# Layer 1's expert rest of 32 rows stacked in one matmul, biases seeded in two copies, splits held and fillers added

## The chip, the cores and the metric

The kernel runs on one core of a Trainium2 chip. The metric is the device time of one execution in microseconds. Three runs of the kernel before took 590.12, 591.79 and 592.01, median 591.79. The engines are named as the profile names them: PE (matmul), ACT (scalar), DVE (vector), POOL (GpSimd), SP (queues DMAs).

## The reference, cut to what matters

The input is 1536 tokens of 256 channels. Two layers follow each other; each is an attention-like block and a mixture of eight experts with two experts per token:

```python
x = x + L0_conv(_ln_c(x)); t = t + L0_ffn(_ln_t(t))      # layer 0
x = x + L1_conv(_ln_c(x)); t = t + L1_ffn(_ln_t(t))      # layer 1
# layer 0's expert e:   y = silu(xf @ w1[e] + b1[e]) @ w2[e] + b2[e]          hidden 1024
# layer 1's expert e:   a, g = split(x @ W1[e] + b1[e], 2)                      2 x 672
#                       y = (a * silu(g)) @ W2[e] + b2[e]                       hidden 672
# out += y * weight of e for the token, for the two chosen experts
```

Everything is float32. The change concerns mostly layer 1's experts, whose hidden width is 672: six times 112, or five times 128 and 32 more.

## The kernel before, in words

Each layer first loads and normalises the tokens, transposes them on PE, computes values and scores, softmax and projection (the conv stage), adds the result to `xres`, normalises again (`xn2`), routes every token to two experts on DVE, and builds tables: 1536 x 2 token rows are sorted by expert into blocks of 128 rows, in layer 1 here 28 blocks. Then a loop runs over the blocks.

A block's rows are gathered from DRAM by POOL (`gather`), transposed on PE (`x_transpose`), and split by ACT and DVE into a high part and a low rest (`xT_hi`, `xT_lo`), since the matmuls run on a shorter float type: each product is three matmuls, high by high, high by low, low by high (`product`, lines 1249 to 1251). All expert weights are split the same way into `w_hi` and `w_lo`. The first three experts of a layer are split ahead of the loop, in 12 pieces, high part by ACT (`high_pieces`, L663) and low part by POOL (L582); later experts within the loop, in pieces, by ACT (L804) and DVE (L1144).

On PE, `step(b)` does in this order: transposes of block b+1's rows; the second product of block b-1 (L1463 on); the transposes of block b's hidden values (`h_transpose`, L1457); the first product of block b+1. In layer 1 the hidden 672 columns are transposed as six tiles of 112, so a second product is 6 x 3 = 18 matmuls of 256 columns. The output bias rides in tile 0 as a 113th row. The first product adds onto PSUM banks which ACT has filled with the bias b1 (`seed`, L794): one copy of 4 x 336 columns in layer 1, which waits until the previous block's `h` is made. Layer 1's first product goes through chunks 2, 3 (the gate g), then 0, 1.

ACT's step: two copies of the transposed hidden values (`hT_hi`), two SiLUs, `xT_hi`, the seed, pieces of the weight split. DVE's step: two `hT_lo`, two products `h_sb` (L1214), `xT_lo`, the block's output `y` (L1231), pieces of the split. POOL's step: gather of block b+2, then scatter-add of block b-1's `y` to DRAM, each scatter waiting for the one before.

PE matmuls on zeros (`keep_busy`, L1257) stand at several places of the routing. At the end of layer 0 the last two blocks are added by one-hot matmuls (`last_rows`, L1504; their one-hots are made on DVE in `last_onehot`, L1184 and L1188), while POOL already splits expert 0 of layer 1 (L582). In each layer's conv stage, DVE multiplies `x_logits` (L1008) before it adds the projected rows (L1016).

## Time and profile before

| what | us |
|---|---|
| median of three runs | 591.79 |
| profiled execution | 593.63 |
| its span | 591.9 |
| PE busy | 544.1 (92%) |
| DVE, ACT, POOL busy | 338.6, 333.3, 280.2 |
| layer 0's loop, first hidden transposes to last | 101 to 284 |
| layer 1's loop, first hidden transposes to last | 389 to 576 |

The profile is of one execution. Busy PE time overstates, since consecutive matmuls overlap; the distance between starts is what one costs in a row of them. A row of the timeline gives start, duration, engine, line, operation, tiles and shape, how many were merged, and in brackets the idle time before it with what ended it.

### The profile page before, as it was taken

Reading aid. Unit: us, or ns where it says so; the run is one execution under the profiler, and the core shown is the slowest. Engines: PE = TensorE matmul, PEld = TensorE weight load, DVE = VectorE, ACT = ScalarE, POOL = GpSimd, SP = SyncE. Lnnn points to the kernel's source line nnn. Section 1 sums busy time; section 2 is a strip of 40 time slices with the busy share of each in tenths; the row PEclk is TensorE's granted clock in tenths of the full one; section 3 lists DMA queues with packets and bytes.
Section 4 is the critical chain, followed back from the end, with each engine's and each line's share of the span. In section 5 each row is a group of like instructions: output and inputs, shape, how many; then the busy total and the mean of one; then the engine's idle time right before and its main releaser. Section 6 shows DMA issues by size and latency. Waiting matters only on the chain.

```text
span 591.9 us, 15435 instructions
## 1 busy us (share of the span) xinstructions
PE 544.1 (92%) x3572; PEld 479.0 (81%) x3573; DVE 338.6 (57%) x719; ACT 333.3 (56%) x605; POOL 280.2 (47%) x331
## 2 busy tenths in 40 slices
PE   7999858999999999999789998699999999999991
PEld 3797525999999989998678874389999999999891
DVE  5448985455544555564884578744655565656330
ACT  3688324566755667665447755254666665666430
POOL 4448214346554466653814260425446555545422
PEclk9799988999999999999999999799999999999996
DMA  7435567455642444235431246532264555322110
GB/s 265 136 107 153 171 210 228 119 150 139 155 83 35 114 123 96 41 88 166 150 100 57 89 144 213 196 120 37 60 193 127 137 137 138 71 76 37 30 27 10
DMA packets 48122, 69.96 MB, mean 118 GB/s; under 512 B 8790, under 2 KB 39648, under 8 KB 48096
## 3 DMA queue, kind: packets, MB, share of 16 engines
q1 hardware_dynamic: 34304, 55.88, 29.4%
q0 software_dynamic: 10464, 13.58, 13.1%
q10 hardware_dynamic: 3328, 0.20, 0.3%
q8 instruction: 12, 0.20, 0.2%
q14 instruction: 14, 0.11, 0.1%
HBM read 57.01 MB, written 13.47 MB: 119 GB/s over the span
## 4 chain that ended last, share of the span: by engine, by line
PE 64%; DMA 13%; DVE 11%; issue 4%; ACT 3%; POOL 3%; POOLq 1%; SPq 0%; DVEq 0%; ACTq 0%
PE banks L1249 14%; PE banks L1251 14%; PE banks L1250 14%; DMA mid_dram<-expert_io,scol 10%; PE banks L1288 5%; PE banks L1457 5%; PE banks L1362 2%; DVE stats L872 2%; PE banks L1426 2%; DVE onehot_row L1095 2%; POOL expert_io L614 2%; PE banks L1257 1%; DVE x_logits L1008 1%; PE banks L1299 1%; DMA xres<-in_x_dram 1%
## 5 line engine op out<-in xcount | busy, mean ns | idle before, releaser
L1249 PE MATMUL banks<-w_hi,xT_hi 128*128 x336 | 119.5, 356 | 4.6 <-DVE xT_lo L1135 2.6
L1249 PE MATMUL banks<-w_hi,hT_hi 128*128 (+2 forms) x392 | 115.8, 295 | 2.0 <-DVE hT_lo L1204 1.3
L1251 PE MATMUL banks<-w_hi,xT_lo 128*128 x336 | 114.9, 342 | 0.0
L1250 PE MATMUL banks<-w_lo,xT_hi 128*128 x336 | 114.3, 340 | 0.0
L1251 PE MATMUL banks<-w_hi,hT_lo 128*128 (+2 forms) x392 | 110.8, 283 | 0.0
L1250 PE MATMUL banks<-w_lo,hT_hi 128*128 (+2 forms) x392 | 110.8, 283 | 0.0
L582 POOL TENSOR_TENSOR w_lo<-raw,w_hi 128x1024 fp32r<-128x1024 f32 (+1 forms) x24 | 62.0, 2604 | 55.8 <-ACT w_hi L663 55.8
L794 ACT COPY banks<-seed_rows 128x1024 f32 (+1 forms) x56 | 64.4, 1151 | 31.0 <-issue 13.5
L1249 PEld LDWEIGHTS banks<-w_hi,hT_hi 128*128 128x128 f32 (+2 forms) x392 | 74.8, 191 | 4.7 <-issue 3.6
L1250 PEld LDWEIGHTS banks<-w_lo,hT_hi 128*128 128x128 f32 (+2 forms) x392 | 75.1, 192 | 0.0
L1251 PEld LDWEIGHTS banks<-w_hi,hT_lo 128*128 128x128 f32 (+2 forms) x392 | 74.9, 191 | 0.0
L602 POOL DMA_INDIRECT expert_io<-xn_dram,gcol x52 | 52.6, 1012 | 41.7 <-POOL gcol L598 40.1
L1204 DVE TENSOR_TENSOR hT_lo<-banks,hT_hi 128x512 fp32r<-128x512 f32 (+1 forms) x112 | 64.4, 616 | 12.2 <-ACT hT_hi L818 7.4
L1249 PEld LDWEIGHTS banks<-w_hi,xT_hi 128*128 128x128 f32 x336 | 63.2, 188 | 8.9 <-issue 5.5
L818 ACT CAST hT_hi<-banks 128x512 fp32r<-128x512 f32 (+1 forms) x112 | 54.1, 535 | 26.1 <-PE banks L1457 23.7
L1251 PEld LDWEIGHTS banks<-w_hi,xT_lo 128*128 128x128 f32 x336 | 63.0, 188 | 4.7
L1250 PEld LDWEIGHTS banks<-w_lo,xT_hi 128*128 128x128 f32 x336 | 63.4, 189 | 3.5
L831 ACT ACTIVATE h_sb<-banks 128x512 f32<-128x512 f32 x56 | 33.5, 599 | 57.0 <-PE banks L1251 57.0
L1144 DVE TENSOR_TENSOR w_lo<-raw,w_hi x40 | 50.3, 1265 | 17.7 <-issue 17.7
L617 POOL DMA_INDIRECT out_dram<-expert_io,scol x27 | 44.1, 1632 | 25.4 <-POOL expert_io L614 23.8
L617 POOL DMA_INDIRECT mid_dram<-expert_io,scol x26 | 43.4, 1670 | 23.1 <-POOL expert_io L614 23.1
L1457 PE MATMUL banks<-ident,h_sb 128*128 128x128 f32 (+1 forms) x392 | 51.9, 272 | 0.0
(206 smaller groups left out, 899.4 us busy)
## 6 DMA issues: line engine op xcount, KB each, us to landing
raw<-in_L_ffn_w_dram SPq DMA_DIRECT2D x32, 512.0 KB, 4.0
raw<-in_L_ffn_W_dram SPq DMA_DIRECT2D x16, 672.0 KB, 4.1
raw<-in_L_ffn_W_dram SPq DMA_DIRECT2D x16, 336.0 KB, 3.8
seed_rows<-in_L_ffn_b_dram SPq DMA_DIRECT2D x8, 672.0 KB
seed_rows<-in_L_ffn_b_dram SPq DMA_DIRECT2D x8, 512.0 KB
xn_dram<-raw SPq DMA_DIRECT2D x6, 512.0 KB, 3.0
wqkv<-in_L_conv_W_qkv_dram SPq DMA_DIRECT2D x2, 768.0 KB, 5.6
mid_dram<-xres SPq DMA_DIRECT2D x3, 512.0 KB, 4.0
```

Source lines behind the costliest of these rows:

```text
L582: pool.tensor_tensor(w_lo[:, e, at], raw[:, 0, at], w_hi[:, e, at].bitcast(F32), ALU.subtract).then_inc(s.pool_split, 1)
L602: pool.indirect_dma_start(out=xg if after(b, 1) else xg_first, out_offset=None, in_=xn_dram, in_offset=bass.IndirectOffsetOnAxis(ap=rows, ...
L617: pool.indirect_dma_start(out=acc, out_offset=bass.IndirectOffsetOnAxis(ap=scol[:, :], axis=0), in_=y_out, in_offset=None, bounds_check=TO ...
L794: nc.scalar.copy(banks[:, 0:f.chunks, 0:f.chunk], seed_row(L, e % SLOTS)[:, 0:f.wide].rearrange("p (c n) -> p c n", c=f.chunks)).then_inc( ...
L818: nc.scalar.copy(hT_hi[0:f.kh, half * j:half * (j + 1), :], bank[4 + j][0:f.kh, 0:half * P].rearrange("p (k s) -> p k s", s=P)).then_inc(s ...
L831: nc.scalar.activation(h_sb[:, f.chunk * j:f.chunk * (j + 1)], bank[j][:, 0:f.chunk], ACT.Silu).then_inc(s.h, 1)
L1144: nc.vector.tensor_tensor(w_lo[:, slot, at], raw[:, (q // PIECES) % 2, at], w_hi[:, slot, at].bitcast(F32), ALU.subtract).then_inc(s.w_lo, 1)
L1204: nc.vector.tensor_tensor(hT_lo[0:f.kh, part, :], bank[4 + j][0:f.kh, 0:half * P].rearrange("p (k s) -> p k s", s=P), hT_hi[0:f.kh, part, ...
L1249: pe.matmul(out, hi, w_high, start=first, stop=False, skip_group_check=onto)
L1250: pe.matmul(out, hi, w_low, start=False, stop=False, skip_group_check=onto)
L1251: return pe.matmul(out, lo, w_high, start=False, stop=last, skip_group_check=onto)
L1457: mm = pe.transpose(bank[4 + j][0:f.kh, k * P:(k + 1) * P], h_sb[:, o:o + f.kh], ident[:, :])
```

## The change

1. Layer 1's hidden width is cut into five tiles of 128 and a rest of 32. The rest's tile is stacked: rows 0 to 31 and 64 to 95 hold the high part, rows 32 to 63 its low rest, rows 96 and 97 ones; the weights beside it hold high, high, low, and the bias as high and low. One matmul of 98 rows then does what three did. `hT_hi`'s two copies take 2 and 4 tiles in place of 3 and 3; DVE repeats the last 32 columns of `h` twice more, and writes the low rows. Each weight piece of the loop's split gets a small second instruction on ACT and on DVE.
2. Layer 1's bias is seeded in two copies of 2 x 336 columns; that for chunks 2 and 3 waits for the SiLUs alone.
3. POOL's splits: pieces 10 and 11 of either layer wait until `x_logits` is made; layer 1's first piece waits for the last one-hot and the end of layer 0's experts.
4. Five matmuls on zeros after the second group of transposes at the start of layer 0.
5. Three more DMAs per expert of layer 1 (the 32 rows three times, the bias row twice); four shared semaphores for the loads of x; register loads moved.

```diff
+BUSY_CHUNK = 5
+HELD_SPLIT = 10
-FFN = [Ffn(wide=1024, kt=8, kh=128, chunk=512), Ffn(wide=1344, kt=6, kh=112, chunk=336)]
+FFN = [Ffn(wide=1024, full=8, tail=0, first_tiles=4, chunk=512), Ffn(wide=1344, full=5, tail=32, first_tiles=2, chunk=336)]
+STACK_LOW, STACK_BIAS_LOW, STACK_ROWS = 64, 96, 98
...
+        def piece_parts(L, q, low):
+            tail_words = C if FFN[L].tail else 0
+            w = (WORDS[L] - tail_words) // PIECES
+            parts = [(slice(0, P), bass.ds((q % PIECES) * w, w))]
+            if tail_words:
+                n = C // PIECES
+                rows = slice(STACK_LOW, STACK_BIAS_LOW + 1) if low else slice(0, STACK_ROWS)
+                parts.append((rows, bass.ds((q % PIECES) * n + PIECES * w, n)))
+            return parts
...
                     pool.wait_ge(s.first_hi, q + 1)
+                    if q == HELD_SPLIT:
+                        pool.wait_ge(x_part, L + 1)
+                    if L == 1 and q == 0:
+                        pool.wait_ge(last_hot, 4)
+                        pool.wait_ge(lay[0].moe_done, 1)
...
-                def seed(b, e):
+                def seed(b, e, pair):
+                    chunks = slice(2 * pair, 2 * pair + 2)
                     act.wait_ge(seed_in, e + (E * L + 1))
                     if after(b, 1):
-                        act.wait_ge(s.h, 2 * b)
+                        act.wait_ge((s.h, s.silu)[pair] if L else s.h, 2 * b)
...
                     if L == 1:
-                        e_next = expert_of(b + 1)
+                        seed(b + 1, e_next, 1)
                         pieces = piece_range(act, b)
                     xT_high(b + 1)
-                    seed(b + 1, e_next)
+                    seed(b + 1, e_next, 0)
...
+                            if f.tail and j == 1:
+                                rows = slice(f.tail, 2 * f.tail)
+                                nc.vector.tensor_tensor(hT_hi[rows, f.full, :], bank[5][rows, 3 * P:4 * P],
+                                                        hT_hi[rows, f.full, :].bitcast(F32), ALU.subtract)
...
+                            if j == 1:
+                                again = STACK_BIAS_LOW // f.tail - 1
+                                nc.vector.tensor_tensor(
+                                    h_sb[:, f.hidden:f.hidden + again * f.tail].rearrange("p (r n) -> p r n", r=again),
...
+                    if L == 0 and j == 1:
+                        keep_busy(BUSY_CHUNK, 6)
...
-                    for k in range(f.kt):
-                        if k % half == 0:
-                            pe.wait_ge(s.hT_lo, 2 * b + 1 + k // half)
-                        rows = f.kh + (f.bias_row if k == 0 else 0)
-                        mm = product(bank[6][:, 0:C], hT_hi[0:rows, k, :], hT_lo[0:rows, k, :], high[0:rows, k, :],
-                                     low[0:rows, k, :], k == 0, k == f.kt - 1)
+                    for k in range(f.full):
+                        for j in range(2):
+                            if k == f.tiles[j].start:
+                                pe.wait_ge(s.hT_lo, 2 * b + 1 + j)
+                        mm = product(bank[6][:, 0:C], hT_hi[:, k, :], hT_lo[:, k, :], high[:, k, :], low[:, k, :],
+                                     k == 0, k == f.kt - 1)
+                    if f.tail:
+                        mm = pe.matmul(bank[6][:, 0:C], hT_hi[0:STACK_ROWS, f.full, :], high[0:STACK_ROWS, f.full, :],
+                                       start=False, stop=True)
```

## Rows read from the trace of the kernel before

**Rows 1.** The page's first two parts: busy time, and granted clock in 40 slices.
```profile
PE 544.1 (92%) x3572; PEld 479.0 (81%) x3573; DVE 338.6 (57%) x719; ACT 333.3 (56%) x605; POOL 280.2 (47%) x331
PEclk9799988999999999999999999799999999999996
```
**Rows 2.** PE's groups by shape: busy us, mean ns, idle before.
```profile
L1249 PE MATMUL banks<-w_hi,hT_hi 113*128 x28 | 10.4, 371 | 0.7 <-issue 0.7
```
**Rows 3.** Timeline of PE, one block of layer 1's loop.
```profile
414.72 0.36 PE L1249 MATMUL banks<-w_hi,hT_hi 113*128 x1
...
416.72 0.28 PE L1250 MATMUL banks<-w_lo,hT_hi 112*128 x1
416.84 0.28 PE L1251 MATMUL banks<-w_hi,hT_lo 112*128 x1
416.96 0.82 PE L1457 MATMUL banks<-ident,h_sb 128*112 128x128 f32 x6
```
**Rows 4.** Timeline of DVE and ACT, a block of layer 1 with two split pieces.
```profile
458.88 2.42 DVE L1144 TENSOR_TENSOR w_lo<-raw,w_hi  x2 [0.44 <-issue]
461.22 1.01 DVE L1204 TENSOR_TENSOR hT_lo<-banks,hT_hi 112x384 fp32r<-112x384 f32 x2
```
**Rows 5.** Timeline of POOL, two scatters of layer 1, eleven blocks apart.
```profile
435.48 1.59 POOL L617 DMA_INDIRECT out_dram<-expert_io,scol  x1 [0.91 <-POOL expert_io L614]
508.22 1.68 POOL L617 DMA_INDIRECT out_dram<-expert_io,scol  x1 [0.91 <-POOL expert_io L614]
```
**Rows 6.** Busy time by stretch of layer 1's loop (us, PE, PEld, DVE, ACT, POOL, PEclk, DMA share, GB/s).
```profile
430.43:505.48 75.05, 75.04 (x553) 73.92 (x552) 44.34 (x77) 47.45 (x78) 41.77 (x56) 1.00 0.55 147
```
**Rows 7.** Timeline of layer 1's blocks 0 to 1: DVE, ACT, PE.
```profile
389.12 0.42 DVE L1135 TENSOR_TENSOR xT_lo<-banks,xT_hi 128x256 fp32r<-128x256 f32 x1 [1.12 <-ACT xT_hi L784]
388.99 1.28 ACT L794 COPY banks<-seed_rows 128x1344 f32 x1
390.58 0.41 PE L1249 MATMUL banks<-w_hi,xT_hi 128*128 x1 [1.24 <-ACT banks L794]
```
**Rows 8.** Timeline of layer 0's conv stage: POOL, DVE, PE.
```profile
46.73 15.69 POOL L582 TENSOR_TENSOR w_lo<-raw,w_hi 128x1024 fp32r<-128x1024 f32 x6 [2.67 <-ACT w_hi L663]
55.73 6.80 DVE L1008 TENSOR_TENSOR x_logits<-x_logits,std 128x96 f32<-128x96 f32 x1
62.87 0.69 DVE L1016 TENSOR_TENSOR xres<-xres,banks 128x512 f32<-128x512 f32 x1
55.93 7.36 PE L1386 MATMUL banks<-wproj,region_b 128*128 128x264 f32 x32 [0.95 <-ACT region_b L757]
71.52 0.68 DVE L1016 TENSOR_TENSOR xres<-xres,banks 128x512 f32<-128x512 f32 x1
```
**Rows 9.** Timeline of PE at the start of layer 0.
```profile
14.19 0.66 PE L1276 MATMUL banks<-ident,region_a 128*128 128x128 f32 x4 [2.33 <-ACT region_a L679]
18.58 3.77 PE L1288 MATMUL banks<-wqkv,region_b 128*96 128x264 f32 x8 [0.68 <-ACT region_b L690]
29.85 2.02 PE L1288 MATMUL banks<-wqkv,region_b 128*96 128x264 f32 x8
```
**Rows 10.** Busy time and granted clock by stretch, there (columns as in Rows 6).
```profile
15.00:16.00 1.00, 0.82 (x5) 0.82 (x6) 0.74 (x4) 1.00 (x4) 0.00 (x0) 0.66 1.08 358
```
**Rows 11.** Timeline of the seam between the layers: POOL, DVE, PE.
```profile
287.12 11.13 POOL L582 TENSOR_TENSOR w_lo<-raw,w_hi 128x1056 fp32r<-128x1056 f32 x4 [1.56 <-ACT w_hi L663]
282.37 1.76 DVE L1188 TENSOR_TENSOR raw<-iota,last_rel 128x1536 f32<-128x1536 f32 x1
287.45 2.17 DVE L1184 SCALAR_TENSOR_TENSOR last_rel<-tile_first,id_sb 128x12 f32<-128x12 f32 x1
289.66 3.95 DVE L1188 TENSOR_TENSOR raw<-iota,last_rel 128x1536 f32<-128x1536 f32 x1
294.05 10.59 PE L1504 MATMUL banks<-raw 128*128 128x256 f32 x40 [2.81 <-DVE raw L1234]
304.75 0.69 DVE L901 TENSOR_TENSOR xres<-xres,banks 128x512 f32<-128x512 f32 x1
```

More of the change, by code:

```diff
@@ L1216, in step @@
                                                     ).then_inc(s.h, 1)
+                            if ahead and after(b, 2):
+                                pieces = (pieces_before(dve, b - 1),) if j == 0 else (pieces[0], pieces_before(dve, b))
                     if ahead:
                         xT_low(b + 1)
-                    if L == 1:
-                        pieces = tables(b, ahead, last)
                     if L == 0 and (last or left == 1):
@@ L1238, in step @@
                         gate_bias(b)
-                    if ahead:
+                    if ahead and after(b, 2):
                         for_pieces(dve, pieces, split)
@@ L1454, in h_transpose @@
                             pe.wait_ge(s.hT_lo, 2 * b - 1 + j)
-                        for k in range(half):
-                            o = (j * half + k) * f.kh
-                            mm = pe.transpose(bank[4 + j][0:f.kh, k * P:(k + 1) * P], h_sb[:, o:o + f.kh],
-                                              ident[:, :])
+                        for k in range(f.tiles[j].start, f.tiles[j].stop):
+                            rows, o = P, (k - f.tiles[j].start) * P
+                            tile = h_sb[:, k * P:(k + 1) * P]
+                            if k == f.full:
+                                rows = STACK_BIAS_LOW
+                                tile = h_sb[:, k * P:k * P + rows]
+                            mm = pe.transpose(bank[4 + j][0:rows, o:o + P], tile, ident[:, :])
                         mm.then_inc(s.hT_mm, 1)
```

146 lines of the change are left out of this document (81 added, 65 removed).

## The prediction, made before the change was run

> **What bounds the kernel now.** I read the busy times first: PE is busy for 544.1 of 591.9 us, at full clock in most slices but the second, which stands at 7 tenths [rows 1]. So PE's own row decides in the loops, and outside them whatever keeps PE waiting. In the loops I read PE's timeline by starts, not by durations: a duration is 0.28 us, but the next matmul starts 0.12 us later [rows 3]. In layer 1 the second product starts at 414.72 and the next transposes at 416.96, so its 18 matmuls take 2.24 us; PE doesn't wait there. Outside the loops three waits stand out. In layer 0's conv stage one small DVE product, `x_logits`, takes 6.80 us [rows 8]. At the seam of the layers PE waits 2.81 us for DVE, whose one-hots took 3.95 us where the first took 1.76 [rows 11]. In the transposes at the start the granted clock goes from 2.4 to 1.2 GHz after PE had waited 2.33 us, and eight value matmuls take 3.77 us where later eight take 2.02 [rows 9, 10].
>
> **The change part by part.** The sum is made against the profiled execution, 593.63 us with a span of 591.9; the median of the runs is 591.79, so 1.84 are taken off at the end.
>
> *A, the held splits of layer 0.* POOL's six splits run from 46.73 to 62.42 back to back, and `x_logits` (both inputs in SBUF) starts at 55.73 and ends at 62.53, 0.11 after the sixth. The first of the six waited behind DVE's long sums; the tile's shortest split is 2.36, so the last two take 4.65 and the fourth ends at 57.77. With pieces 10 and 11 held, POOL stops there; `x_logits` ends at 57.9 in place of 62.53, and adding starts at 58.2 in place of 62.87: 4.65 earlier. What is late next is PE: its projection delivers a pair of tiles every 7.36/4 = 1.84 us from 55.93, so the sixth pair is there at 55.93 + 6 x 1.84 = 67.0, and DVE takes it at 67.1 in place of 71.52. The gain is 4.4 us. The held pieces end at 62.9, before DVE's next product of two SBUF operands, about 5 us after adding begins. The chain behind (statistics, routing, tables) is DVE's and moves as a whole. Bounds: 3.9 (one such collision) to 4.65. In layer 1 the hold has no wait to remove, since PE delivers its first pair there 2 us after `x_logits`: 0.
>
> *B, the fillers.* Five matmuls of 512 columns take 5 x 0.43 = 2.1 us at the low clock and half of it at the full one, estimated from the 512-column matmuls on zeros that stand before this place (9.05 us for 32 there, 0.28 each, some at either clock). They stand in the 2.33 us in which PE waits for ACT [rows 9], so they delay nothing. If the clock stays up, the last twelve transposes are done before ACT's six copies, which end 0.3 sooner, and the eight value matmuls take 1.9 in place of 3.77. That is 2.2 us, and PE is the chain from there on. If the clock falls in spite of them: 0. Value taken 2.2, bounds 0 and 2.2.
>
> *C, the seam.* POOL's four splits of layer 1 start at 287.12, and DVE's two one-hot instructions meet them: 2.17 and 3.95 us in place of about 0.2 and 1.76 [rows 11]. Now POOL waits for both. The one-hots are ready at 289.4, and DVE's last output needs the second product, which ends at 290.4; it starts then and not at 293.53, 3.1 us earlier. PE no longer idles 2.81 us, so I take it that the clock stays up and the forty matmuls (10.59 us, less if nothing slows them) keep ahead of DVE. DVE adds the first pair at 292.1 (the tiles of x land at 291.8, so no earlier), then runs without a wait: six times 1.49, three times 0.38 and two times 0.35, and reaches the last pair at 301.0 in place of 304.75 [rows 11]. That is 3.8. Against it: the splits now run from 289.5 to 299.9, across DVE's add-and-normalise, which has one product of two SBUF operands per four tiles (`less_mean`). One falls at 297.1, into the small stacked split. I take 0.5 for it and 3.3 for C. Bounds: 0.6 (it waits out a split, 2.7 as a first bad case) and 3.8. What is behind POOL: the loads of expert 1 wait for its pieces and go 1 to 2.4 us later, and ACT splits that expert 20 us later; hidden.
>
> *D, the loop of layer 1.* Two matmuls fewer per second product, at 0.12 each [rows 3], in 28 blocks [rows 2]: 28 x 0.24 = 6.7 us. The number of transposes stays six. The matmul of 98 rows has 256 columns like those of 112 and 128, which all show 0.12. Of what is added, DVE's repeat (64 columns) and low rows (32 x 128) are 0.2 to 0.3 each, and stand while PE is in its 3.78 us of first product; in blocks without a split DVE has more than a microsecond to spare there, so they cost nothing. ACT's copies of 2 and 4 tiles sum to the same as 3 and 3. Two things eat into it. First, split pieces: 20 of them, mostly two per block, and DVE's second instruction nets 0.1 each (0.16 for the smallest, less 0.07 for 64 columns fewer). In such a block DVE begins `hT_lo` at 461.22, right after the splits [rows 4], and PE needs the first part at 461.85, so 0.1 to 0.2 per block come through: 1.0. Second, POOL's scatters: where expert weights are loaded they come 72.74/11 = 6.61 us apart [rows 5], and PE took 6.82 per block [rows 6]. At 6.58 PE would be faster than POOL, and what POOL lags is stall once its slack of 1.8 us is used: 1.0. D is 4.7. Bounds: 6.7, and 0.1 if those eleven blocks give nothing and each piece costs 0.2.
>
> *E, the seed.* In block 1 PE waits 1.24 us for ACT's copy of 1344 columns, which began at 388.99 [rows 7]. Now the copy for chunks 2 and 3 is done in front of `xT_hi`, and PE waits for `xT_lo`, which ends at 389.54: it starts at 389.65 in place of 390.58, 0.9 us. The second copy, estimated at 0.72 (1.28 us for 1344 columns and 1.02 for 1024), is ready well before chunk 0. In later blocks PE doesn't wait for seeds, so 0. Bounds 0.5 and 0.95.
>
> The extra DMAs take SP 0.35 us each behind its other issues, and nothing waits for them within a microsecond: 0.
>
> Sum: 4.4 + 2.2 + 3.3 + 4.7 + 0.9 = 15.5. 593.63 - 15.5 = 578.1; less 1.84 it is 576.3.
>
> **Two rules weighed.** For A and C the rows show a DVE instruction with both operands in SBUF standing still while POOL reads SBUF, 6.80 us across three of POOL's splits in one place, and 2.17 to the end of one split in another [rows 8, 11]. The Trainium skill (SBUF — State Buffer, "Who interferes with whom") says that the shared ports are locked exclusively for a whole instruction by whoever comes first. By that rule alone `x_logits` would have got in at the first split's end, at 57.8, and A would be worth nothing; the row shows it starved to 62.53, so I go by the row. The same rule speaks against C: `less_mean` could wait out a split, which is the third rival below.
>
> For B the rows show the clock falling while PE was busy again, after the wait [rows 9, 10]. The Trainium skill (TensorE: Matmul & The Clock Gate, "What's actually happening") says that the monitor runs free of the kernel's start, so the same gap may cost in one execution and not in another. By the page B would be a mean between 0 and 2.2.
>
> **The rivals.**
> - *The clock falls all the same.* The fillers cover 1.1 us of a 2.33 us wait if PE is at full clock, and 1.2 remain. Then B is 0: 578.5. Chance 0.14. For it: the gap isn't closed. Against it: PE's wait of 1.24 us in layer 1's block 1 [rows 7] left its slice of the page at 9 tenths, the twenty-seventh [rows 1].
> - *Something else bounds layer 1's loop.* POOL's scatter chain and DVE's split blocks take over, D is 1 in place of 4.7: 580.0. Chance 0.16. For it: 6.61 against 6.58. Against it: only eleven of the blocks are such; elsewhere POOL waits for DVE's output.
> - *The held splits hurt where they now run.* `less_mean` at the seam and in layer 0 waits out a split: C is 0.6 and A 3.9, together 3.2 lost: 579.5. Chance 0.11.
> - *The hold doesn't do what it says*: `x_logits` is late for another reason (its DMA lands at 55.5, so at most 2 us), A is 0 to 2: 579.7. Chance 0.03.
> - *Slower than before:* the stacked tile comes late in every block. The second part of `hT_lo` now follows a copy of 4 tiles on ACT and two instructions on DVE. If it reached PE 0.7 us after the seventh matmul of each second product, 28 blocks would lose 19.6 and gain D's 6.7: with A, B, C and E, 593.63 - 10.8 + 12.9 - 1.84 = 593.9. It decides from a stall of 0.62 per block on. Against it: it takes a delay of 3 us in blocks without a split. Chance 0.03.
> - The forecast has the remaining 0.53.
>
> **How the numbers follow.** The tops of the terms sum to 4.65 + 2.2 + 3.8 + 6.7 + 0.95 = 18.3, 573.5; their bottoms to 3.9 + 0 + 0.6 + 0.1 + 0.5 = 5.1, 586.7. Both ends at once are unlikely; with 1.5 us for the runs' own spread below, 572 to 583 holds all cases but the slower one and combinations of two rivals. A difference under 0.3% (1.8 us) can't be told from none. Faster 0.96, same 0.01, slower 0.03.
>
> **What would show it.** A: `x_logits` near 2.2 us long in layer 0, and POOL's splits in two groups. B: granted clock 1.00 from 15 to 22 us, eight value matmuls in 2.0. C: no wait of PE before the one-hot matmuls and full clock there; `less_mean` short. D: 0.24 less from transposes to transposes in undisturbed blocks; 16 matmuls per second product; in split blocks, whether PE waits for `hT_lo`. E: PE's wait for the bias copy gone in block 1. I'd be wrong if the loop's blocks shrink by less than 0.15 on average, or if a wait on POOL's split appears in layer 1's conv stage.

## The result, and the profile after

The changed kernel takes 584.76 us (median, 582.9 to 585.86) where the kernel before took 591.53 beside it: a ratio of 0.9877 [0.984, 0.9914]. Run again on another chip (6 runs) it took 584.46 against 589.94, 0.9891 [0.9843, 0.9938]. It is faster, by 6.8 and 5.5 us between the medians (1.1 to 1.2%) and not by the 15.5 forecast; 576.3 is missed, and so is the range, whose upper end was 583.

The profiled execution took 584.26 us with a span of 582.5. Its page, first two parts, against [rows 1]:

```profile
PE 536.6 (92%) x3521; PEld 473.9 (81%) x3522; DVE 346.9 (60%) x795; ACT 340.5 (58%) x652; POOL 276.9 (48%) x333
PEclk9999979999999999999989999899999998899996
```
PE is busy 7.5 us less, the second slice's clock is up from 7 to 9, and two slices within the loop of layer 1 (481 to 510 us) are down to 8. That last thing is new.

Layer 0's conv stage, timelines of PE, POOL and DVE, against [rows 8, 9]:

```profile
18.07 2.10 PE L1337 MATMUL banks<-wqkv,region_b 128*96 128x264 f32 x8 [1.36 <-ACT region_b L717]
...
44.55 11.05 POOL L609 TENSOR_TENSOR w_lo<-raw,w_hi 128x1024 fp32r<-128x1024 f32 x4 [2.67 <-ACT w_hi L690]
56.17 4.68 POOL L609 TENSOR_TENSOR w_lo<-raw,w_hi 128x1024 fp32r<-128x1024 f32 x2 [0.56 <-ACT w_hi L690]
...
53.50 2.22 DVE L1041 TENSOR_TENSOR x_logits<-x_logits,std 128x96 f32<-128x96 f32 x1
56.05 0.69 DVE L1051 TENSOR_TENSOR xres<-xres,banks 128x512 f32<-128x512 f32 x1
```
The eight value matmuls take 2.10 in place of 3.77, POOL's splits stand in a group of four and one of two, `x_logits` takes 2.22 in place of 6.80, and adding starts 6.8 us earlier; A and B together were to give 6.6. The first hidden transposes of layer 0 come 7.4 us earlier (93.61 and 100.98).

The seam, timelines of POOL, DVE and PE, against [rows 11]:

```profile
282.14 7.21 POOL L609 TENSOR_TENSOR w_lo<-raw,w_hi 128x1056 fp32r<-128x1056 f32 x3 [3.79 <-DVE raw L1223]
...
280.24 1.76 DVE L1223 TENSOR_TENSOR raw<-iota,last_rel 128x1536 f32<-128x1536 f32 x1
...
289.58 0.66 DVE L917 SCALAR_TENSOR_TENSOR less_mean<-mean_var,rstd 128x4 f32<-128x4 f32 x1
293.58 0.69 DVE L934 TENSOR_TENSOR xres<-xres,banks 128x512 f32<-128x512 f32 x1
...
282.82 9.66 PE L1559 MATMUL banks<-raw 128*128 128x256 f32 x44
```
POOL waits for the one-hots, which take 1.76; one `less_mean` takes 0.66 against 0.16 for its fellows. The last pair is added at 293.58 and not at 304.75, which is 16.6 us behind layer 0's last hidden transposes and not 20.4. Layer 1's first hidden transposes start at 377.43 and before at 388.52: 11.1 us ahead, of which 7.4 were there at the end of layer 0's loop, so C is 3.7 here.

The next hidden transposes start at 384.80 and 396.76, 12.0 us ahead. The 0.9 that this block adds is E and one second product, which is 0.25 shorter by D, together. PE's timeline, against [rows 7], shows E by itself:

```profile
378.87 0.42 PE L1296 MATMUL banks<-w_hi,xT_hi 128*128 x1 [0.62 <-ACT banks L825]
```
PE starts 1.44 us after its transposes where it was 2.06, so E is 0.6, and a wait of 0.62 stays. The last hidden transposes start at 566.58 and 575.80: only 9.2 ahead. The loop of layer 1, which was to give 4.7, took 2.7 back.

It isn't the blocks as such. Timeline of PE, starts of the hidden transposes in undisturbed blocks, against [rows 3]:

```profile
404.24 0.82 PE L1510 MATMUL banks<-ident,h_sb 128*128 128x128 f32 x6
410.72 0.82 PE L1510 MATMUL banks<-ident,h_sb 128*128 128x128 f32 x6
417.20 0.82 PE L1510 MATMUL banks<-ident,h_sb 128*128 128x128 f32 x6
```
They come 6.48 us apart, where it was 6.73. But between 443 and 511 few are undisturbed, and the last five of the loop (7.05 to 7.4) are hardly shorter than before. PE's waits in the loop after its second block, first of the kernel before (396 to 576), then of the changed one (384 to 567): us in total, times, longest.

```profile
PE banks L1426 <- issue: 0.7, 1, 0.7
PE banks L1249 <- issue: 0.4, 1, 0.4
```
```profile
PE banks L1475 <- DMA expert_io<-xn_dram,gcol: 3.7, 3, 2.7
PE banks L1296 <- DVE hT_lo L1244: 1.3, 3, 0.7
PE banks L1475 <- issue: 1.1, 3, 0.6
```
The worst block of the changed kernel (timelines of PE, POOL, DVE and SP; then the stretch behind the wait: us, busy, granted clock, DMA share, GB/s):

```profile
485.16 0.82 PE L1510 MATMUL banks<-ident,h_sb 128*128 128x128 f32 x6
492.43 0.69 PE L1475 MATMUL banks<-ident,expert_io 128*128 128x128 f32 x2 [2.75 <-DMA expert_io<-xn_dram,gcol]
496.33 1.48 PE L1510 MATMUL banks<-ident,h_sb 128*128 128x128 f32 x6
...
484.38 1.60 POOL L644 DMA_INDIRECT out_dram<-expert_io,scol  x1 [0.91 <-POOL expert_io L641]
486.99 1.55 POOL L629 DMA_INDIRECT expert_io<-xn_dram,gcol  x1 [0.81 <-POOL gcol L625]
...
486.45 1.19 DVE L1178 TENSOR_TENSOR w_lo<-raw,w_hi  x1 [0.41 <-issue]
487.66 0.22 DVE L1178 TENSOR_TENSOR w_hi<-raw,w_hi  x1
487.91 0.43 DVE L1244 TENSOR_TENSOR hT_lo<-banks,hT_hi 128x256 fp32r<-128x256 f32 x1
...
487.91 0.35 SPq L440 DMA_DIRECT2D seed_rows<-in_L_ffn_b_dram  x1
...
491.00:499.00 8.00, 6.57 (x31) 0.57 0.15 40
```
The block takes 11.17 us. POOL issues the scatter late, and so the gather behind it; the gather's issue takes 1.55 us (1.01 elsewhere) and ends at 488.54, after a bias load of 672 KB went out at 487.91; PE waits 2.75 us for its rows, and then the granted clock is 0.57 on average over eight microseconds, near the lower of its two levels, 1.2 GHz. It is what happened behind the wait of 2.33 us in [rows 9, 10], in another place. The Trainium skill (TensorE: Matmul & The Clock Gate, "What's actually happening") says that the clock follows how busy PE has been of late; the trace agrees, the fall standing right behind the wait of 2.75 us.

### The profile page after: what moved, and what is told of

Read it like the earlier page. It is cut to its first block, busy times and chain, and to the rows that moved or that the text cites. A ratio compares the mean times of both kernels' runs of the same rounds, so it can differ in the third digit from the quotient of the medians.

```text
span 582.5 us, 15620 instructions
## 1 busy us (share of the span) xinstructions
PE 536.6 (92%) x3521; PEld 473.9 (81%) x3522; DVE 346.9 (60%) x795; ACT 340.5 (58%) x652; POOL 276.9 (48%) x333
## 4 chain that ended last, share of the span: by engine, by line
PE 68%; DVE 11%; DMA 7%; issue 5%; ACT 3%; POOL 2%; DVEq 1%; POOLq 1%; SPq 0%; ACTq 0%
PE banks L1296 15%; PE banks L1298 15%; PE banks L1297 15%; PE banks L1510 6%; PE banks L1337 5%; DMA out_dram<-expert_io,scol 4%; PE banks L1411 2%; DVE stats L905 2%; PE banks L1475 2%; DVE onehot_row L1130 2%; PE banks L1348 1%; PE banks L1304 1%; DMA xres<-in_x_dram 1%; ACT region_a L706 1%; DVE xres L1051 1%
## 5 line engine op out<-in xcount | busy, mean ns | idle before, releaser
L1296 PE MATMUL banks<-w_hi,hT_hi 128*128 x364 | 109.0, 300 | 2.9 <-DVE hT_lo L1244 2.7
L1297 PE MATMUL banks<-w_lo,hT_hi 128*128 x364 | 103.5, 284 | 0.0
L1298 PE MATMUL banks<-w_hi,hT_lo 128*128 x364 | 103.5, 284 | 0.0
L825 ACT COPY banks<-seed_rows 128x672 f32 (+1 forms) x84 | 69.0, 822 | 29.2 <-issue 14.4
L609 POOL TENSOR_TENSOR w_lo<-raw,w_hi 128x1024 fp32r<-128x1024 f32 (+2 forms) x24 | 58.8, 2467 | 52.0 <-ACT w_hi L690 44.9
L1296 PEld LDWEIGHTS banks<-w_hi,hT_hi 128*128 128x128 f32 x364 | 70.0, 192 | 6.5 <-issue 5.4
L629 POOL DMA_INDIRECT expert_io<-xn_dram,gcol x52 | 53.8, 1034 | 41.9 <-POOL gcol L625 39.4
L846 ACT CAST hT_hi<-banks 128x512 fp32r<-128x512 f32 (+1 forms) x112 | 55.5, 535 | 28.6 <-PE banks L1510 25.4
L1297 PEld LDWEIGHTS banks<-w_lo,hT_hi 128*128 128x128 f32 x364 | 70.3, 193 | 0.0
L1298 PEld LDWEIGHTS banks<-w_hi,hT_lo 128*128 128x128 f32 x364 | 70.2, 193 | 0.0
```

What stands on the lines that cost most here:

```text
L609: pool.tensor_tensor(w_lo[:, e, at], raw[:, 0, at], w_hi[:, e, at].bitcast(F32), ALU.subtract).then_inc(s.pool_split, 1)
L629: pool.indirect_dma_start(out=xg if after(b, 1) else xg_first, out_offset=None, in_=xn_dram, in_offset=bass.IndirectOffsetOnAxis(ap=rows, ...
L825: nc.scalar.copy(banks[:, chunks, 0:f.chunk], seed_row(L, e % SLOTS)[:, 0:f.wide] .rearrange("p (c n) -> p c n", c=f.chunks)[:, chunks, :] ...
L846: nc.scalar.copy(hT_hi[:, part, :], bank[4 + j][:, 0:(part.stop - part.start) * P] .rearrange("p (k s) -> p k s", s=P)).then_inc(s.hT_hi, 1)
L1296: pe.matmul(out, hi, w_high, start=first, stop=False, skip_group_check=onto)
L1297: pe.matmul(out, hi, w_low, start=False, stop=False, skip_group_check=onto)
```

## The experiments

All with the kernel before beside them on their chip. "Loop" is the time from the second to the last start of hidden transposes in layer 1, of the profiled execution: 179.0 before, 181.8 after. A period or block is the time from one such start to the next; the first is 7.36 us after the change, the following six 6.48.

**1. Everything but the stack**: the kernel before with holds, fillers and the seed in two copies, its second product as it was.

```diff
+                    if q == HELD_SPLIT:
+                        pool.wait_ge(x_part, L + 1)
+                    if L == 1 and q == 0:
+                        pool.wait_ge(last_hot, 4)
...
+                    if L == 0 and j == 1:
+                        keep_busy(BUSY_CHUNK, 6)
...
+                        seed(b + 1, e_next, 1)
```

> The kernel before with the holds, the fillers and the two seed copies, and layer 1's six tiles of 112 as they were. Of the 7.4 us that the whole change gained in its profiled stages up to layer 1's first blocks came 12, and the rest of layer 1's loop gave 9 back that two matmuls less should have gained or left. Theory M (a faster PE runs into POOL's chain of scatters and gathers, or into DVE's fuller split blocks): this kernel is as fast as the changed one or faster, 579 to 584, with blocks of 6.73 us and few longer ones. Rival R (the stacked tile earns its 0.24 per block and what was lost is chance of one execution): this kernel is 4 to 6 us slower than the changed one, 589 to 590.

584.39, 0.9879 [0.984, 0.9919]; loop 177.4, blocks 6.73. The same time as the whole change, within some 3 us by the two intervals: the stack as a whole is worth nothing.

But this kernel differs from the changed one at the seam too. POOL's fourth split there isn't cut in two by the stack's small one, and `less_mean` waits until POOL's row of splits ends. Timelines of POOL and DVE:

```profile
283.81 9.57 POOL L589 TENSOR_TENSOR w_lo<-raw,w_hi 128x1056 fp32r<-128x1056 f32 x4 [2.69 <-DVE raw L1202]
...
291.23 2.18 DVE L896 SCALAR_TENSOR_TENSOR less_mean<-mean_var,rstd 128x4 f32<-128x4 f32 x1
```
It takes 2.18 us where the changed kernel's took 0.66, and the last pair is added 18.1 us behind the end of layer 0's loop and not 16.6. So it is in all six changed kernels here without the small split, and in none with it. The stack thus brings 1.5 us at the seam, and since it is worth nothing as a whole, it loses about as much in the loop by the medians, with the same uncertainty of 3 us; in the profiles the loop is 4.4 and 5.6 us longer with the stack (181.8 and 183.0 against 177.4). The other parts give 7.2 us here, and would give some 8.7 with a short `less_mean`.

**2. Only a shorter second product**: the same, with the last tile's two cross matmuls left out of layer 1, 16 per second product, and nothing added on DVE, ACT or the queues.

```diff
+                        if f.bias_row and k == f.kt - 1:
+                            mm = pe.matmul(bank[6][:, 0:C], hT_hi[0:rows, k, :], high[0:rows, k, :],
+                                           start=False, stop=True)
```

> without_stack, and in layer 1 the last tile's two cross matmuls (high by low, low by high) left out: PE's second product is as short as in the changed kernel (16 matmuls), without any added work on DVE, ACT or in the DMAs. Theory P (POOL's scatter and gather chain bounds a faster PE): undisturbed blocks of 6.49, long ones in the middle of the loop waiting for the gather, total within 1.5 us of the changed kernel. Theory V (DVE's and ACT's added split work is the loss): the full 6.7 us under without_stack, no waits for hT_lo beyond those of before.

585.29, 0.9882 [0.9838, 0.9926]; loop 177.9, blocks 6.49, but one of 7.63 and one of 10.31, PE waiting for the gather in both. Nothing that the stack adds is needed to lose its gain; a shorter period is enough.

**3. The changed kernel without the second split instructions** on ACT and DVE, for layer 1's experts 3 to 7 (the stacked tile's weights are left unsplit).

```diff
-                    for rows, at in piece_parts(L, q, 0):
+                    for rows, at in piece_parts(L, q, 0)[0:1]:
...
-                    for n, (rows, at) in enumerate(piece_parts(L, q, 1)):
+                    for n, (rows, at) in enumerate(piece_parts(L, q, 1)[0:1]):
```


> The changed kernel; for layer 1's experts 3 to 7 the stacked tile's weights are not split (the second small instruction of each piece on ACT and on DVE is left out, so the tile's weights are stale). Theory V: the waits for hT_lo behind the row transposes (0.33 to 0.6 us in five blocks) go, 2 to 3 us faster. Theory P: the waits for the gather stay, less than 2 us.

581.53 (576.04 to 583.27), 0.9802 [0.9752, 0.9851]; loop 177.6. The waits for `hT_lo` are gone, the gather's stay (blocks of 7.51 and 10.02).

**4. The changed kernel with fewer bytes**: only 64 of the 1344 columns of each half of W1 are loaded for layer 1's experts 4 to 7; the others keep what an earlier expert left there.

```diff
+                    if L == 1 and e > SLOTS and part < 2:
+                        to, src = to[:, 0:64], src[:, 0:64]
                     sp.dma_start(to, src).then_inc(done, 16)
```


> The changed kernel; for layer 1's experts 4 to 7 only the first 64 of 1344 columns of W1 are loaded, so 1.3 MB less of DMA per expert (weights otherwise stale). Theory P with DMA traffic as its cause (scatters and gathers land late beside weight loads): scatters come under 6.3 us apart all through, no wait for a gather, layer 1's loop shorter by 5 to 7 us. Theory V: less than 1 us.

579.01, 0.9772 [0.9731, 0.9813]; loop 175.0. The other way round: the gather's waits are gone, those for `hT_lo` stay (2.0 us in 5 over the loop).

**5. to 7. Each of the other parts taken out of the changed kernel.**

```diff
-                    if q == HELD_SPLIT:
-                        pool.wait_ge(x_part, L + 1)
```


> The changed kernel without the hold on pieces 10 and 11: POOL's six splits of layer 0 run back to back again. If starvation by POOL's splits is what made x_logits late (term A), x_logits is 6.8 us long again and the first xres addition is 4.65 us later than in the changed kernel; all behind it moves as a whole, so 584.8 becomes about 589.2 (588 to 590). Rival (the hold does nothing, x_logits was late by its DMA): x_logits stays near 2.2 us and the time stays within 1 us of 584.8. Second rival (what is won early is lost in layer 1's loop, because the phase of the loop against the loads decides): the addition is 4.65 later but the end only 0 to 2 us.

589.0 (12 runs), 0.9926 [0.9887, 0.9966]. `x_logits` takes 6.86 again, adding starts at 59.87 in place of 56.05. The first hidden transposes of layer 0 come 4.3 us later. By the medians A is 4.2 us, though single runs go from 583.0 to 593.3.

```diff
-                    if L == 1 and q == 0:
-                        pool.wait_ge(last_hot, 4)
+                    if L == 1 and q == 3:
```


> The changed kernel with POOL's wait for the one-hots (last_hot) left out and only the wait for the end of layer 0 (moe_done) kept, moved to the fourth piece as it was before the change. If term C holds, the two one-hot instructions take 2.2 and 3.9 us again, PE waits 2.8 us in front of the one-hot matmuls, and layer 1's first hidden transposes come 3.3 to 3.7 us later: 588.1 to 588.5. Rival (the splits now run across DVE's add-and-normalise and cost there what they saved): 584.8 within 1 us, transposes at most 1 us later.

589.17 (12 runs), 0.9958 [0.9928, 0.9989]. Timelines of DVE and PE there:

```profile
281.70 2.18 DVE L1218 SCALAR_TENSOR_TENSOR last_rel<-tile_first,id_sb 128x12 f32<-128x12 f32 x1
283.92 3.94 DVE L1222 TENSOR_TENSOR raw<-iota,last_rel 128x1536 f32<-128x1536 f32 x1
288.31 8.90 PE L1558 MATMUL banks<-raw 128*128 128x256 f32 x40 [2.81 <-DVE raw L1280]
```
The one-hots and PE's wait are as before the change [rows 11]; the forty matmuls take 8.90 and not 10.59, at a granted clock of 1.00 from 291 to 299. The second transposes of layer 1 come 3.6 us later than in the changed kernel's first profile, but 1.7 of that is there already at the end of layer 0's loop (278.61 and 276.95), which this edit doesn't touch. Counted from there the last pair is added 2.6 us later (19.2 and 16.6) and the first hidden transposes of layer 1 come 1.9 later. C is 2 to 2.6 by this trace, and 4.4 by the medians.

```diff
-                    if L == 0 and j == 1:
-                        keep_busy(BUSY_CHUNK, 6)
```


> The changed kernel without the five filler matmuls in layer 0's transposes. If the clock falls there whenever PE waits, granted clock 0.66 from 15 to 16 us, eight value matmuls in 3.77 us and 2.2 us more: 587.0. Rival (whether the clock falls at this gap differs from one execution to the next, so that term B is a mean between 0 and 2.2): between 584.8 and 587.0, and the profiled execution may show the clock at 1.00. Second rival: no effect on the median even with the clock low, since DVE and not PE is waited for behind it: 584.8.

586.47, 0.9887 [0.9842, 0.9932]: 1.7 us more by the medians, while the ratio is the same as the changed kernel's 0.9877 and 0.9891. So the size of B rests on the traces. The profiled execution took 591.15, so only its start is used here; PE's timeline:

```profile
14.12 0.66 PE L1323 MATMUL banks<-ident,region_a 128*128 128x128 f32 x4 [2.33 <-ACT region_a L706]
15.11 2.13 PE L1323 MATMUL banks<-ident,region_a 128*128 128x128 f32 x12 [0.33 <-ACT region_a L706]
17.99 3.84 PE L1335 MATMUL banks<-wqkv,region_b 128*96 128x264 f32 x8 [0.75 <-ACT region_b L717]
```
The wait, the low clock and the 3.8 us are back, and adding starts 2.2 us later (58.21).

In all three profiled executions the eighth period of the loop took 10.5 us, which in the changed kernel's first profile took 6.56. So these medians may hold more than the part taken out, and the parts aren't summed from them.

**8. POOL's chain shorter.** In each scatter the wait for the copied indices stands behind the copy of the rows.

```diff
-                    pool.wait_ge(s.scol, b + 1)
                     pool.wait_ge(s.e_sb, b + 1)
                     pool.tensor_copy(y_out, y_sb(b)).then_inc(s.y_moved, 1)
+                    pool.wait_ge(s.scol, b + 1)
                     pool.wait_ge(s.y_moved, b + 1)
```


> The changed kernel with one of POOL's waits in each scatter moved: the wait for the copied indices (scol) stands behind the copy of the rows (y_out) and not in front of it. It takes the 0.22 us gap between the two copies out of POOL's chain, whose part from one landing to the next issue is 1.71 us where it lags. If POOL's chain of scatters and gathers prices layer 1's loop (each block there 0.2 shorter for POOL, and the lag that makes the gathers late is not built up), PE's waits for the gather shrink from 9.4 us to under 4 and the time is 581 to 583. Rival (the late gather comes from one meeting of a gather with DVE's split and a seed load, whatever POOL's lag is): the wait stays above 7 us in all and the time is 584 to 585.

579.97, 0.9807 [0.9768, 0.9846]. The time is below the expected 581 to 583, but the trace doesn't show what was expected of it: PE still waits 3.3 us for gathers, in two blocks, and the changed kernel's two profiles have 3.7 and 4.9 (the 9.4 of the expectation is in neither). What neither this profile nor the next shows is the long eighth period. Again, on another chip:

> The stacked kernel with POOL's wait for the copied indices behind the copy of the rows, once more on another chip: 580.0 came from one chip, and the same move without the stack gave 582.7 on a second. If the move is worth 4 to 5 us with the stack wherever it runs, the ratio to the kernel before is 0.978 to 0.984 again. If it was of its chip: 0.986 to 0.99, as for the changed kernel.

580.65, 0.9792 [0.9748, 0.9837]. It holds: this kernel is faster than the changed one, and than the one without the stack.

**9. DVE's split in front of y**, alone and with the move of experiment 8.

```diff
                     if ahead:
                         xT_low(b + 1)
+                    if L == 1 and ahead and after(b, 2):
+                        for_pieces(dve, pieces, split)
```


> The changed kernel with one move on DVE in layer 1's loop: the split pieces of a block stand in front of the scaling of y (behind xT_lo) and no longer behind it. DVE waits there for nothing but ACT's piece, which ends about 0.7 us after the hidden transposes begin, so the split runs some 0.7 to 0.9 us earlier, and hT_lo with it. In the traces so far a gather's issue on POOL is stretched (1.01 to 1.5-2.0 us, to 0.86-0.89 us after the end of DVE's split) each time it begins while DVE's split of raw and w_hi is running, and never when it begins first. If term D was lost to these two things, hT_lo's waits go (2.4 us), a gather that lags by 1.6 us now begins after the split, and the time is 579 to 582. Rival (what costs is the late landing of the scatter and gather behind the expert's loads, the stretched issue being small beside it): only hT_lo's part comes back, 582 to 583.5. Second rival (the later y starves POOL's scatter of its rows): 585 or more.

583.63, 0.9857 [0.9828, 0.9887]. No gather is stretched any more and the clock no longer falls in the loop, as hoped. But the waits for `hT_lo`, which were to go, take 3.3 us in 4 and those for gathers 1.8 in 3, and POOL's waits (395 to 555) show the mechanism of the second rival, though not its price: the rows of y come late, block after block (changed kernel first, then this one).

```profile
POOL expert_io L641 <- DVE region_b L1278: 8.6, 12, 2.0
```
```profile
POOL expert_io L641 <- DVE region_b L1280: 20.3, 17, 3.0
```
Five blocks of 6.8 to 6.9 and four of 7.7 to 8.3 take the place of the longest.

> Both: POOL's wait for the copied indices behind the copy of the rows (580.0 by itself) and DVE's split in front of y. If the two act on different waits (POOL's lag, and hT_lo's lateness) they add: 577 to 578.5. If they remove the same stalls, 580 within 1 us.

583.65, 0.9855 [0.9828, 0.9883]: neither expectation holds; with y late, a shorter way behind y's wait is worth nothing and the gain of experiment 8 is gone.

**10. The stack in two matmuls** of 65 rows: 17 per second product, no second split instruction.

```diff
+                        pe.matmul(bank[6][:, 0:C], hT_hi[0:STACK_ROWS, f.full, :], high[0:STACK_ROWS, f.full, :],
+                                  start=False, stop=False)
-                        mm = pe.matmul(bank[6][:, 0:C], hT_hi[0:STACK_ROWS, f.full, :], high[0:STACK_ROWS, f.full, :],
+                        mm = pe.matmul(bank[6][:, 0:C], hT_hi[0:STACK_ROWS, f.full, :], low[0:STACK_ROWS, f.full, :],
```

> The changed kernel with the last tile stacked in another way: 65 rows [high; low; one] against w_hi and then against w_lo, so 17 matmuls per second product and not 16, no second instruction in DVE's and POOL's split of the last piece, one DMA less per expert. Undisturbed blocks 6.60 (half of what the stack saves). If DVE's extra 0.2 us in split blocks is what makes hT_lo late, those waits fall from 2.4 to under 1 us and the time is 582 to 584, better than the full stack although PE has more to do. If PE's own row decides, it is 28 x 0.12 = 3.4 us slower than the full stack less the removed waits: 585 to 587.

585.05, 0.9887 [0.9853, 0.9922]. The waits for `hT_lo` are gone, the late gathers stay (blocks of 7.76 and 9.54). Without the small second split `less_mean` takes 2.18 us at the seam again, so 1.5 of the time is lost there. With the move of experiment 8:

> The stack in two matmuls of 65 rows (17 per second product, no second split instruction) together with the moved wait on POOL. Blocks of 6.62 leave POOL 0.14 more per block than 6.48 and hT_lo isn't late, so with the shorter POOL chain the late gathers may go: 579 to 581, level with or below the full stack with the moved wait. Rival (the meeting of a gather with DVE's split stays, as it did in two_mm): 582 to 584.

580.59, 0.9809 [0.9756, 0.9863], level with experiment 8 alone, though the same 1.5 us are lost at the seam.

**11. The bias loads later.**

```diff
-                    sp.wait_ge(s.w_lo, PIECES * e + 1)
+                    sp.wait_ge(s.w_lo, PIECES * e + (3 if L else 1))
```


> The changed kernel with layer 1's last two bias loads (672 KB each) on SP waiting for two more split pieces, so that they no longer go out right behind a lagging gather. If the bias load is what makes the gather near 487 land 5 us after its issue, the wait of 2.7 us and the fall of the clock behind it go, and the time is 581 to 582.5. Rival (the gather is late because POOL lags and its issue is stretched, whichever load is under way): the stall stays, 584 to 585.5; it may move to a neighbouring block.

585.87, 0.99 [0.9858, 0.9941]. The stall of 11 us near 487 is gone, but the loop isn't shorter (182.9): the eighth block takes 9.35 and two later ones 8.61 and 10.04, and PE waits twice, up to 2.1 us, for the seed's copy, which is now late. It doesn't tell a bias load's share from POOL's lag.

**12. The same cuts without the stack, and both at once with it**, on one chip with the changed kernel again.

> The changed kernel once more, on the chip of the three kernels beside it, since its time so far (584.8) is of four runs. Expected 584 to 586.

584.46, as above.

> The kernel with every part of the change but the stack (584.4), and with POOL's wait for the copied indices behind the copy of the rows, as in the run that brought the stacked kernel to 580.0. If POOL's chain limits only the shorter blocks of the stack, this changes nothing here: 584 to 585, and with it the stack is worth 4 us. If the shorter chain helps whatever PE's period is (or the 580.0 was of its chip), it is 580 to 582, and the stack is worth nothing here either.

582.69, 0.9863 [0.9821, 0.9904]: between the two expectations. Without the stack the moved wait brings 0.9 (by the ratios) to 1.7 us (by the medians); with it, 3.8 to 5.9. With the moved wait the stack is then worth 2.0 to 4.2 us, and 1.5 of it is the seam's.

> The kernel with every part of the change but the stack, with only 64 of 1344 columns of each half of W1 loaded for the experts 4 to 7 of layer 1; the output is wrong for it. With the stack the same cut brought 5.8 us (579.0). If it is the loads' traffic behind late scatters and gathers that takes what the stack's shorter blocks would give, it brings little here, where the blocks of 6.73 hardly wait for a gather: 583.5 to 584.4, and the stack is worth 4.5 to 5.5 us of its 6.7 without this traffic. Rival (the loads cost the loop the same with and without the stack): 578.5 to 580, and the stack is worth nothing without them either.

583.54, 0.9887 [0.9846, 0.9928]: next to nothing, where the same cut brought 5.8 with the stack. The rival falls.

> The stacked kernel with both kinds of stall taken away: few columns of W1 loaded for the experts 4 to 7 of layer 1, and the second split instructions of the experts 3 to 7 left out; the output is wrong for both. Alone they brought 5.8 and 3.2 us. If term D is lost to just these two, all but the last four blocks of layer 1 take 6.48 to 6.6 us, and the time is 575.5 to 577. If they overlap: 578 to 579.

575.56 (574.47 to 576.84), 0.9747 [0.9708, 0.9786]; loop 172.4, all blocks up to the last five but one (6.93) within 6.48 to 6.55. Stretch 430 to 500, PE (us, busy, granted clock, DMA share, GB/s), changed kernel first, then this one:

```profile
430.00:500.00 70.00, 65.97 (x455) 0.95 0.50 128
```
```profile
430.00:500.00 70.00, 69.86 (x513) 1.00 0.41 93
```
With both kinds of stall gone the kernel is 8.0 us faster than its counterpart without the stack (583.54). That is more than D's upper bound of 6.7, so it isn't all D: 1.5 is the seam's `less_mean`, and layer 0's loop, which is the same code, took 184.2 and 185.1 us in the two profiles. In the profiles the time from the first to the last hidden transposes of layer 1 is 179.7 and 185.0, so D is 5.2. It isn't 6.7 because the last five periods (6.71 to 7.28 here) are almost as long with the stack as without it. With the stalls gone D is there wherever it can be, so the two kinds of stall are what it was lost to.

## Where the long block comes from

The same program, two executions: the eighth period of the loop took 6.56 us in the changed kernel's first profile and 10.44 in its second. Timelines of POOL, DVE, SP and (second) PE, first and second:

```profile
425.14 1.01 POOL L629 DMA_INDIRECT expert_io<-xn_dram,gcol  x1 [0.81 <-POOL gcol L625]
...
425.13 1.23 DVE L1178 TENSOR_TENSOR w_lo<-raw,w_hi  x1 [0.55 <-issue]
...
426.63 0.91 SPq L474 DMA_DIRECT2D raw<-in_L_ffn_W_dram  x2
```
```profile
423.69 0.18 POOL L638 COPY scol<-scatter_tab 128x1 int32 x1 [3.38 <-DMA out_dram<-expert_io,scol]
...
428.00 1.81 POOL L629 DMA_INDIRECT expert_io<-xn_dram,gcol  x1 [0.81 <-POOL gcol L625]
...
427.73 1.19 DVE L1178 TENSOR_TENSOR w_lo<-raw,w_hi  x1 [0.57 <-issue]
...
429.18 0.91 SPq L474 DMA_DIRECT2D raw<-in_L_ffn_W_dram  x2
...
433.20 0.69 PE L1475 MATMUL banks<-ident,expert_io 128*128 128x128 f32 x2 [2.42 <-DMA expert_io<-xn_dram,gcol]
```
In both POOL is behind, since the scatter before lands late beside the first loads of the next expert, and the gather is issued only after the next scatter. The first profile shows such a scatter with what followed its landing, then one at the end of the loop, where no load is under way:

```profile
413.20 1.64 POOL L644 DMA_INDIRECT out_dram<-expert_io,scol  x1 [0.91 <-POOL expert_io L641]
420.83 0.18 POOL L638 COPY scol<-scatter_tab 128x1 int32 x1 [3.12 <-DMA out_dram<-expert_io,scol]
...
554.81 1.60 POOL L644 DMA_INDIRECT out_dram<-expert_io,scol  x1 [0.92 <-POOL expert_io L641]
558.88 0.18 POOL L638 COPY scol<-scatter_tab 128x1 int32 x1 [2.46 <-DMA out_dram<-expert_io,scol]
```
That is 7.6 us from issue to landing against 4.1, and with few columns of W1 loaded (experiment 4) POOL's wait of 3.12 is 1.21. In the first execution the gather begins with DVE's split, 0.01 us apart, and takes 1.01. In the second it begins 0.27 after it, and its issue ends 0.89 us after the split's end; PE waits, and the clock falls.

The held issue is not all of PE's wait. A load that waits for DVE's split is let go on SP when the split is done, so a gather that the split has held gets out behind that load: in the first execution the loads follow the gather's issue by 0.48 us, and its rows are there in time, within 1.9 us of the end of the issue; in the second they precede that end by 0.63 us, and the rows are there 3.4 us after it. Over the profiles of all the kernels with the shorter second product 25 gathers of layer 1's loop began when a split of DVE had run for 0.08 us or more; all took 1.52 to 2.07. None of the others did, those that began ahead of the split or with it included. In 9 of the 25 no load went out meanwhile: the rows were there 1.8 to 1.9 us after the end of the issue, and the block took 7.4 to 7.8 us. In the other 16 a load had gone out 0.6 to 0.9 us before that end: the rows came 3.4 to 3.9 us after it, PE waited 2.3 to 2.75 us, and the block took 9.2 to 9.5 us where the granted clock stayed up (7 of the 16) and 10.0 to 11.2 where it fell (9). In the kernel before, and in all the kernels with blocks of 6.73, the gathers that met a split began 0.3 to 0.9 us ahead of it. DVE's split moves with PE, POOL's gather with the landings: 0.25 us less per block for PE, and the split gets in ahead of a gather that lags.

That the split holds up the issue, and that the load in front delays the rows, are read from the traces' order in time. No kernel was run that took DVE's second SBUF operand away, and none in which only the order of load and gather was changed; experiment 11 comes nearest, but its gather at 488.73 wasn't held at all.

## Why the prediction was wrong, step by step

- **A, right.** 4.4 forecast; the first addition 6.8 earlier together with B (6.6 forecast), and 3.8 to 4.2 when taken out. POOL's splits stand in two groups.
- **B, right by the traces.** Granted clock 1.00 from 15 to 16 us with the fillers (0.66 before [rows 10]), the low clock and 2.2 us back without them. The forecast case, not the rival of the clock. The ratios of the runs don't tell the two kernels apart.
- **C, right.** 3.3 forecast, 3.7 between the two profiles and 2 to 4.4 when taken out: `less_mean` lost 0.5 in one place, as allowed for. The third rival, in which it waits out a split, came true where the small stacked split is missing (2.18 us, experiment 1). One thing was wrong: the clock still falls at 297 to 301 (0.57), so full clock behind the seam was not kept.
- **E, a third too large**: 0.9 forecast, 0.6 measured (2.06 to 1.44 us in front of block 1's product; without the stack the first period goes from 8.25 to 7.66). PE's wait there was to be gone, and 0.62 of it stay.
- **D's first line, right in the undisturbed blocks**: 0.25 less each. But it was counted for 28, and the last five periods gain almost nothing; 5.2 us is what it gives when nothing is in its way (experiment 12). The prediction's own sign of being wrong was a gain under 0.15 per block; the loop's periods grew by 0.1 on average.
- **The step that failed is D's second deduction**: "Second, POOL's scatters: where expert weights are loaded they come 72.74/11 = 6.61 us apart", priced at 1.0. The row gave an average over eleven blocks, and the forecast treated POOL as an engine that is a few hundredths slower than PE. It is a chain that falls behind at single blocks, when a scatter lands late, and makes it up in the following ones. Against 6.73 its slack held; against 6.48 it makes up less, the gather behind the late scatter meets DVE's split from the wrong side, and a block with such a meeting takes 7.4 to 7.8 us against 6.48, and 9.2 to 11.2 where a load goes out ahead of the gather as well. The changed kernel's two profiles have one and two blocks of 10.4 to 11.2, at 4.0 to 4.7 us each, against the 5.2 that the shorter blocks could give. Cutting the loads of W1, which make the scatters late, brought 5.8 us (experiment 4).
- **D's first deduction, too small.** The second split instructions were priced at 1.0 and cost 3.2 by the medians (experiment 3; its runs spread over 7 us). The instruction is 0.22 us, where 0.16 was forecast for the smallest, but PE's wait it causes is up to 0.7, and that PE's delay reaches the next meeting of a gather with a split is likely, not shown. Together with the above D is 0 with the 1.5 of the seam in it, about -1.5 in the loop alone (experiment 1, within some 3 us), and not 4.7.
- **The rival "Something else bounds layer 1's loop" was the right one**, at a chance of 0.16 and with D put at 1. It gave 580.0, and the range ended at 583 since no case in it had the loop longer than before. What spoke against it there, that only eleven blocks are such, was no help: one or two of them were enough.
- **The sum of the other terms.** 10.8 was forecast for A, B, C and E. The profiled pair shows 11.7 (12.0 less D's first 0.25), but the medians of experiment 1 only 7.2 [4.8, 9.5], and with the 1.5 us that this kernel lacks at the seam 8.7 [6.3, 11.0]. That interval holds the forecast, so no shortfall of these terms is shown. Part of the difference is the profiled pair itself: layer 0's loop took 183.3 to 183.4 us in it and 184 to 185.4 in most other profiles, whose edits don't touch it. It isn't known which execution of the kernel before is typical, as its runs go from 587 to 599.

## What to carry to other kernels

A loop whose bound engine, once relieved, is 2% faster than a chain of DMAs (6.48 against 6.61 us per block) need not give what the engine is relieved of: look in the trace for the blocks in which the chain falls behind and ask in what time it recovers, not for its average. Price a wait of PE with the granted clock behind it: blocks with much the same wait took 9.2 to 9.5 us where it stayed up and 10.0 to 11.2 where it fell. When a part of a change is left out to price the rest, look in the trace whether the other stages stayed as they were; here the stack's small split was worth 1.5 us in a place where nobody had counted it. And where a shorter period saves little, try the slack of the neighbour: moving one wait on POOL by 0.2 us made the changed kernel 4 us faster (580.0 and 580.7), more than the stack had given.

## What was not expected of the hardware

- A gather's issue on POOL takes 1.01 us, and 1.5 to 2.1 when it begins during a DVE `tensor_tensor` with two operands in SBUF; it then ends 0.88 to 0.89 us after DVE's instruction. The Trainium skill (SBUF — State Buffer, "Who interferes with whom") says that such an instruction contends with GpSimd's reads, and infers that descriptor generation, which needs the write interface, is not held up by it. Here the issue of a DMA whose row numbers stand in SBUF is held up.
- When the two begin 0.01 us apart neither loses more than 0.04 us (1.01 and 1.23). In the two executions above a difference of 0.3 us in the order goes with one of 3.9 us in the block.
- A scatter, 256 columns of 128 rows with an add, landed 7.6 us after its issue began beside loads of 672 KB, and 4.1 us after it without them.
- A gather's rows were there 1.8 to 1.9 us after the end of its issue when no load went out meanwhile, and 3.4 to 3.9 us when one had gone out 0.6 to 0.9 us before that end.
